# Layer-0 output projection and gate transposes moved to the two transpose banks, probabilities in two buffers, orders laid anew

## The chip, the cores and the metric

One core of one Trainium2 chip runs the whole program. The time is device microseconds of one execution, lower is better. The engines are TensorE (PE), VectorE (DVE), ScalarE (ACT), GpSimd (POOL) and the queue engine SyncE (SP). They run side by side, each takes its instructions strictly in the order in which they were written, and they wait for one another on semaphores. TensorE writes its results to PSUM, of which this kernel uses eight banks of 512 float32 columns.

## The reference

Four sequences of 512 tokens, 128 channels, and a context of 77 tokens for each. Two layers, all in float32, here with the names of the steps in the kernel:

```python
# layer 0, attention over the context: 16 heads of 8
q = LN(x) @ Wq.T + bq;  k, v = ctx @ Wk.T + bk, ctx @ Wv.T + bv        # hstats hnorm hturn hq
p = softmax(q k^T / sqrt(8))                                            # s mx sub exp
x = x + (p v) @ Wo.T + bo                                               # ta tb tc, v nm, ot op x
# layer 0, second half: attention among the 4 sequences, 4 heads of 32, then a mixture of 8 experts
z = LN(x);  z = z + MHA_over_the_batch(z);  y = LN(z) * g1 + b1         # zturn q qk dot soft wv tot mturn proj res ynorm
gates = softmax(y @ wg);  e = argmax;  place in e's queue, cap 256      # yturn lg gdiff gate places cap
x = x + LN(y + gate * (y @ w1[e] + b1[e]) @ w2[e] + ...) * g2 + b2      # load turn moe total norm2
# layer 1, attention over the context with the 32 largest scores of each head
s = LN(x) Wq1 ctx Wk1                                                   # lturn ask scores keep
p = softmax(s where s >= 32nd largest);  x = x + p ctx                  # max mark dif cut exp sign product, turn copy value norm add3
# layer 1, token-shifted channel mixing
z = LN(x);  out = x + sigmoid(mix_r(z) W_r) * (relu(mix_k(z) W_k)^2 W_v)   # fturn shift up acts down half end
```

## The kernel before

The 2048 tokens are 16 tiles of 128. Layer 0's attention and the part among the sequences go by `j` (0 to 3), the quarter of the sequence, with the four sequences together, since a token attends to the same position of the other three. Inside `attend(j)` a tile has the number `u = 4 j + b`. Everything later goes by tile `t` (0 to 15). `ORDER` is one list of some 2200 words such as `v1@2` (step `v1` at index 2), written out by hand or by a tool. Each engine's block goes through that list (`run`) and issues those steps that belong to it. So the list fixes the order on every engine. What may not run yet waits on a semaphore (`hold`).

The names that matter here:

- `psS` is four PSUM banks with the scores. `psT[:, 0]` and `psT[:, 1]` are the two transpose banks. `psM0` and `psM1` are the last two.
- In `attend`, `s{b}` makes the scores, `mx{b}` and `sub{b}` (DVE) take the maximum and subtract it, `exp{b}` (ACT) makes `e0`. `ta`, `tb`, `tc` transpose `e0` in ten pieces into the banks of `psT`, `ca`, `cb`, `cc` (ACT) copy them to `pT`, and `v{b}` multiplies them with the values into `psM0`. `nm{b}` (DVE) divides, `ot{b}` transposes the result, `oT{b}` copies it, `op{b}` is the output projection and `x{b}` (DVE) adds it to `x1`. Before the change `ot` and `op` write to `psM0` too, so `m0_free` lets the next `v`, `hturn` or `hq` into `psM0` only when `x{b}` is done (`x1_made`).
- `among(j)` works in `psM1`: `zturn`, `q0` to `q3`, `mturn`, `proj`, then `yturn`, `lg` and `places` for the gates. `zturn` of the next `j` waits for `gates_set`, the last of them.
- `topk(t)` on DVE is 16 steps `max..` and 12 steps `mark..` of four heads each. It finds the 32 largest of 77 scores per head. `keep@t` (ACT) brings the scores of tile `t` to it, from a ring of four buffers. `cut`, `dif` and `product` (POOL) and `exp`, `sign` (ACT) make the probabilities, `turn0` to `turn2` and `value` multiply them, `norm@t` (DVE) inverts the denominators.
- `mix(t)` is `fturn`, `shift`, `up`, `acts`, `down`, `fvalue`, `half`, `end`. Its work lies in `psT[:, 1]`.
- `fill@k` is two matmuls of ones on a mask row, into `psT[:, 1]`, whose result nobody reads. There are 420 of them, spread over the list.

Statistics of the layer norms on DVE use the tiles `stats`, `mv`, `veps`, `rstd` under a key `x` or `m`. The two norms of `among` share the key `m`.

## Time and profile before

| | us |
|---|---|
| median of 3 runs | 541.65 |
| fastest, slowest of them | 537.23, 545.12 |
| span of the profiled execution | 543.1 |
| DVE busy in it | 477.4 (88%) |
| PE busy in it | 471.0 (87%) |
| ACT, POOL busy | 294.5, 263.8 |

The profiled execution is one of its own. Its span is counted from its first to its last instruction; its time on the device's counter isn't listed. The span lies inside the range of the three times and 1.45 us above their median. Busy times are those in which at least one instruction of the engine was under way. On PE they hold the fills too.

### The profile page before, as it was taken

To read this page: it belongs to the slowest core of one execution; us is meant where nothing else is said; L and a number is where in the kernel's file an instruction comes from. 1 tells how busy PE (TensorE), PEld (TensorE's weight loads), DVE (VectorE), ACT (ScalarE), POOL (GpSimd) and SP (SyncE) were. 2 spreads that over 40 slices of the span, in tenths; PEclk is the share of its full clock that TensorE was granted. 3 is DMA by queue.
4 is the path that set the end of the run, shared out by engine and by line. 5 is a ranking of instruction groups with operands and counts; after the bars stand their busy time and mean duration, and the time that the engine had idled before them with its cause. 6 is when DMAs were issued, how large, how long until landed. Compare 5 with 4: busy or idle time off the path is not lost. (4 is left out here: it accounts for less than half of the span.)

```text
span 543.1 us, 12113 instructions
## 1 busy us (share of the span) xinstructions
PE 471.0 (87%) x3161; PEld 347.3 (64%) x3161; DVE 477.4 (88%) x3011; ACT 294.5 (54%) x812; POOL 263.8 (49%) x403
## 2 busy tenths in 40 slices
PE   4999999898986999799889898999889989689485
PEld 3578877566755765467657666667657757566374
DVE  5784679959879899899989999999999999999972
ACT  1143551433444335424777788787786887635343
POOL 4320120500323435634685687777668667736622
PEclk9999999979998999899999999999999998989957
DMA  8700000000000000000000000000000000000000
GB/s 278 301 2 1 2 1 2 0 1 0 2 2 0 2 2 1 1 1 2 7 1 8 7 2 2 10 2 2 11 1 2 7 7 7 2 5 8 6 5 11
DMA packets 5938, 9.68 MB, mean 18 GB/s; under 512 B 744, under 2 KB 4976, under 8 KB 5616
## 3 DMA queue, kind: packets, MB, share of 16 engines
q1 hardware_dynamic: 5584, 8.35, 4.3%
q8 instruction: 28, 0.46, 0.4%
q10 hardware_dynamic: 288, 0.56, 0.3%
q14 instruction: 38, 0.31, 0.2%
HBM read 7.86 MB, written 1.05 MB: 16 GB/s over the span
## 5 line engine op out<-in xcount | busy, mean ns | idle before, releaser
L1318 PE MATMUL psT<-mrow,mones 128*128 128x308 bf16 x840 | 131.3, 303 | 5.0 <-ACT vv L672 4.3
L939 DVE MAX8 top<-area_b 128x8 f32<-128x77 f32 x768 | 116.0, 290 | 0.0
L1318 PEld LDWEIGHTS psT<-mrow,mones 128*128 128x128 bf16 x840 | 83.6, 101 | 41.2 <-issue 14.7
L947 DVE MATCH_REPLACE8 area_b<-top,area_b 128x77 f32<-128x77 f32 x512 | 109.1, 293 | 0.0
L947 DVE MATCH_VALUE_LOAD area_b<-top,area_b 128x8 f32 x512 | 74.2, 150 | 0.0
L947 DVE MATCH_REPLACE8 area_b<-top,area_a 128x77 f32<-128x77 f32 x256 | 54.7, 286 | 0.0
L1088 PE MATMUL psM<-vblk,pT 128*128 128x135 f32 (+3 forms) x320 | 42.4, 288 | 5.2 <-ACT early L562 3.0
L1088 PEld LDWEIGHTS psM<-vblk,pT 128*128 128x128 f32 (+1 forms) x320 | 39.7, 197 | 8.9 <-issue 7.2
L420 POOL TENSOR_TENSOR p<-area_b 128x1232 f32<-128x1232 f32 x15 | 41.9, 2792 | 6.9 <-issue 3.3
L1286 PE MATMUL psM<-vblk,pT 128*128 128x135 f32 (+3 forms) x320 | 43.5, 292 | 1.5 <-ACT pT L631 0.8
L1286 PEld LDWEIGHTS psM<-vblk,pT 128*128 128x128 f32 (+1 forms) x320 | 41.2, 203 | 5.1 <-issue 4.3
L319 POOL TENSOR_TENSOR rstd_m<-veps_m,expo 128x4 f32<-128x4 f32 x8 | 8.1, 1018 | 74.7 <-DVE veps_m L689 74.4
L581 ACT ACTIVATE mparts<-psM,cur 128x128 f32<-128x128 f32 x128 | 38.1, 369 | 9.8 <-PE psM L1225 9.6
L939 DVE MAX8 top<-area_a 128x8 f32<-128x77 f32 x256 | 38.3, 285 | 5.0 <-ACT area_a L609 5.0
L1269 PE MATMUL psT<-consts,p 128*128 128x128 f32 (+1 forms) x160 | 29.0, 299 | 14.6 <-POOL p L420 8.9
L413 POOL TENSOR_TENSOR area_b<-area_a,top 128x1232 f32<-128x1232 f32 x15 | 34.0, 2266 | 12.0 <-DVE top L939 9.9
L406 POOL TENSOR_TENSOR dif<-area_a,top 128x1232 f32<-128x1232 f32 x16 | 36.3, 2268 | 4.6 <-DVE top L939 4.6
L947 DVE MATCH_VALUE_LOAD area_b<-top,area_a 128x8 f32 x256 | 35.5, 143 | 0.0
L716 DVE TENSOR_REDUCE mx<-psS 128x16 f32<-128x1232 f32 x16 | 23.0, 1438 | 13.5 <-PE psS L1059 13.4
L1233 PE MATMUL psM<-mparts,consts 128*128 128x128 f32 x288 | 34.8, 275 | 0.0
L1269 PEld LDWEIGHTS psT<-consts,p 128*128 128x128 f32 (+1 forms) x160 | 18.3, 146 | 25.2 <-POOL p L420 11.3
L1233 PEld LDWEIGHTS psM<-mparts,consts 128*128 128x128 f32 x288 | 33.4, 192 | 0.0
(223 smaller groups left out, 1015.0 us busy)
## 6 DMA issues: line engine op xcount, KB each, us to landing
area_a<-in_w1T SPq DMA_DIRECT2D x1, 2064.0 KB, 11.0
area_b<-in_w SPq DMA_DIRECT2D x1, 2048.0 KB, 15.4
x<-in_x SPq DMA_DIRECT2D x4, 256.0 KB, 6.9
out<-fin SPq DMA_DIRECT2D x16, 64.0 KB, 1.5
rows<-in_rows SPq DMA_DIRECT2D x1, 576.0 KB, 6.7
vblk<-in_vblk SPq DMA_DIRECT2D x1, 540.0 KB, 15.6
weights<-in_weights SPq DMA_DIRECT2D x1, 516.0 KB, 6.5
consts<-in_consts ACTq DMA_DIRECT2D x1, 392.5 KB, 3.9
```

The lines of the kernel that those rows point to most:

```text
L406: e.tensor_tensor(dif[:], scores_sb[t % RING][:], top[:, t % 2, 0, :, 0, None].broadcast_to([P, H, KEYS]), ALU.subtract)\
L413: e.tensor_tensor(cut, scores_sb[t % RING][:], top[:, t % 2, TOPK // 8 - 1, :, 7, None].broadcast_to([P, H, KEYS]), ALU.subtract)\
L420: e.tensor_tensor(p1.rearrange("p (h k) -> p h k", k=KEYS), ex1, cut, ALU.mult).then_inc(s["p_set"], 1)
L581: ins = e.activation(mparts[:, x_], psM0[:, at + (x_ - lo) * D:at + (x_ - lo + 1) * D], ACT.Copy, scale=cur[:, D + x_:D + x_ + 1])
L716: e.tensor_reduce(mx0.rearrange("p (g i) -> p g i", g=G), scores_ps, AX, ALU.max).then_inc(s["s_max"], 1)
L939: ins = e.max(tops[:, r, h], (left if r else scores_sb[t % RING])[:, h])
L947: ins = e.match_replace(left[:, h], tops[:, r, h], (left if r else scores_sb[t % RING])[:, h], GONE)
L1088: ins = mm(streams(psM0, c), pT[0:w, c], vblk0[0:w, b, c, None, :].broadcast_to([w, copies(c)[0], VB]), start=(c == 0), stop=(c == NCH - 1 ...
L1233: ins = mm(psM0[:, 0:D], ident, mparts[:, x_], start=False, stop=(x_ == E))
L1269: ins = tr(psT[0:w, 0, (c % 4) * P:(c % 4 + 1) * P], p1[:, c * P:c * P + w], ident)
L1286: ins = mm(streams(psM1, c), pT1[0:w, c], vblk1[0:w, t // NJ, c, None, :].broadcast_to([w, copies(c)[0], VB]), start=(c == 0), stop=(c == ...
L1318: mm(bank[:, 0:B * KEYS], mones[:], mrow.rearrange("p b k -> p (b k)"), start=True, stop=True)
```

## The change

1. `ot{b}` and `op{b}` write to `psT[:, 1]` (columns 256 and 384) and no longer to `psM0`, and `x{b}` reads there. `psM0` is free for the next user when `nm{b}` has read the product (`pv_norm`).
2. `yturn`, `lg` and `places` write to `psT[:, 0]` and no longer to `psM1`. The copy of the transposes goes to a tile of its own, `yT`. `zturn` of the next `j` waits for `m_res`, the residual, and no longer for the gates.
3. `pT` has two buffers, so `ca` and `cb` wait for the product of the tile before the last and no longer for the last.
4. The waits for the transpose banks stand in two functions, `t0_free` and `t1_free`. All users of such a bank wait for all earlier ones: `tb`, `ot`, `op`, `fturn` and `fill` for the adds `x{b}`, `ta` and `turn0` for the gates.
5. The norm of `ynorm` has tiles of its own (key `y`), and one semaphore counts the three steps of the statistics. In `gdiff` two instructions change places.
6. `FILLS` is 355 and no longer 420, and `ORDER` is another list. In front of `max00@0`, the first top-k step, it has 8 fills, where the old one had 55. The numbers of all other instructions stay the same.

```diff
-FILLS = 420
+FILLS = 355
...
+STATS = 2 * B + 1
...
-        for n in ("x", "m"):
+        for n in ("x", "m", "y"):
...
-        pT = sb("pT", [P, NCH, P])
+        pT = sb("pT", [P, 2, NCH, P])
...
+        yT = sb("yT", [P, B, P])
...
         def m0_free(e, step):
             hold(e, s["h_xnT"], begun(step, "hturn"))
             hold(e, s["h_qT"], begun(step, "hq"))
-            hold(e, s["x1_made"], begun(step, "v0", "v1", "v2", "v3"))
+            hold(e, s["pv_norm"], begun(step, "v0", "v1", "v2", "v3"))
             hold(e, s["n2_out"], begun(step, "turn"))
+
+        def t0_free(e, step):
+            hold(e, s["t_copiedA"], 3 * begun(step, "ta0", "ta1", "ta2", "ta3"))
+            hold(e, s["p_copied"], 3 * begun(step, "turn0"))
+            hold(e, s["y_T"], begun(step, "yturn"))
+            hold(e, s["g_d"], begun(step, "lg"))
+            hold(e, s["gates_set"], begun(step, "places"))
+
+        def t1_free(e, step):
+            projected = begun(step, "op0", "op1", "op2", "op3")
+            hold(e, s["x1_made"], projected)
+            if projected < NT:
+                hold(e, s["t_copiedB"], begun(step, "tb0", "tb1", "tb2", "tb3"))
+                hold(e, s["o_T"], begun(step, "ot0", "ot1", "ot2", "ot3"))
+            hold(e, s["f_vv"], begun(step, "fturn"))
...
                     def first():
-                        hold(e, s["pv_made"], u)
+                        hold(e, s["pv_made"], u - 1)
                         hold(e, s["t_turned"], 3 * u + 1)
-                        e.activation(pT[:, 0:4].rearrange("p c n -> p (c n)"), psT[:, 0], ACT.Copy).then_inc(s["t_copiedA"], 1)
+                        e.activation(pT[:, u % 2, 0:4].rearrange("p c n -> p (c n)"), psT[:, 0], ACT.Copy).then_inc(s["t_copiedA"], 1)
...
+                def upright():
+                    hold(e, s["y_turned"], j + 1)
+                    hold(e, s["lg_made"], j)
+                    e.activation(yT[:], psU, ACT.Copy).then_inc(s["y_T"], 1)
...
-                        e.tensor_tensor(x1[:, t], psM0[:, 384:512], x1[:, t], ALU.add).then_inc(s["x1_made"], 1)
+                        e.tensor_tensor(x1[:, t], psT[:, 1, 384:512], x1[:, t], ALU.add).then_inc(s["x1_made"], 1)
...
                     def oturn():
                         hold(e, s["pv_norm"], u + 1)
-                        tr(psM0[:, 256:384], at0[:], ident).then_inc(s["o_turned"], 1)
+                        t1_free(e, f"ot{b}@{j}")
+                        tr(psT[:, 1, 256:384], at0[:], ident).then_inc(s["o_turned"], 1)
 
                     def project():
                         hold(e, s["o_T"], u + 1)
-                        mm(psM0[:, 384:512], at0T[:], Wt["wo0"], start=True, stop=True).then_inc(s["o_proj"], 1)
+                        t1_free(e, f"op{b}@{j}")
+                        mm(psT[:, 1, 384:512], at0T[:], Wt["wo0"], start=True, stop=True).then_inc(s["o_proj"], 1)
...
                 def zturn():
                     if j == 0:
                         e.wait_ge(s["b12_stored"], 1)
-                    hold(e, s["gates_set"], j)
+                    hold(e, s["m_res"], j)
                     hold(e, s["q_z"], B * j + B)
                     turn4(psM1, zt, s["q_turned"])
...
-ORDER = """hstats@0 masks@0 hrstd@0 kblk1@0 hnorm@0 vb0@0 kblk@0 hturn@0 vb1@0 keys@0 hT@0 bias@0 vm0@0 hq@0 hstats@1 hqT@0 s0@0 vm1@0 hrstd@1
+ORDER = """hstats@0 hrstd@0 hnorm@0 masks@0 bias@0 hturn@0 kblk@0 hT@0 vb0@0 kblk1@0 hq@0 hstats@1 vb1@0 keys@0 hqT@0 vm0@0 hrstd@1 wmix@0
```

Three places of the order. The first is PE at its start. L1112 (after: L1136) spreads the values of layer 0, L1031 (L1055) transposes the normalised tokens, L1043 (L1067) makes the queries, L1056 and L1059 (L1080, L1083) the scores, L1318 is a fill. Before:

```order
L1112 MATMUL psM<-vsrc,consts 128x4x24 x5
L1031 MATMUL psM<-consts,xn 128x128 x4
L1112 MATMUL psT<-vsrc,consts 128x4x24 x5
L1043 MATMUL psM<-hT,early 128x512
L1056 MATMUL psS<-kblk,hT 128x308 x4
L1059 MATMUL psS<-mrow,mones 128x308 x4
L1318 MATMUL psT<-mrow,mones 128x308 x18
L1056 MATMUL psS<-kblk,hT 128x308 x4
L1059 MATMUL psS<-mrow,mones 128x308 x4
```

After:

```order
L1055 MATMUL psM<-consts,xn 128x128 x4
L1136 MATMUL psM<-vsrc,consts 128x4x24 x5
L1067 MATMUL psM<-hT,early 128x512
L1136 MATMUL psT<-vsrc,consts 128x4x24 x5
L1080 MATMUL psS<-kblk,hT 128x308 x4
L1083 MATMUL psS<-mrow,mones 128x308 x4
L1055 MATMUL psM<-consts,xn 128x128 x4
L1067 MATMUL psM<-hT,early 128x512
L1080 MATMUL psS<-kblk,hT 128x308 x4
L1083 MATMUL psS<-mrow,mones 128x308 x4
```

The transposes and the queries moved ahead of the spreading, those of the second quarter stand where the 18 fill matmuls stood. The second place is PE at the end of quarter 1 of the attention. L1088 (L1110) is the product `v`, L1095 (L1118) is `ot`, L1099 (L1123) is `op`, L1077 (L1099) the transposes of `e0`. Before:

```order
L1088 MATMUL psM<-vblk,pT 128x5x27 x6
L1056 MATMUL psS<-kblk,hT 128x308 x4
L1059 MATMUL psS<-mrow,mones 128x308 x4
L1077 MATMUL psT<-consts,e 128x128
L1077 MATMUL psT<-consts,e 80x128
L1095 MATMUL psM<-consts,at 128x128
L1318 MATMUL psT<-mrow,mones 128x308 x4
L1099 MATMUL psM<-early,at0T 128x128
L1318 MATMUL psT<-mrow,mones 128x308 x6
L1088 MATMUL psM<-vblk,pT 128x3x27 x2
```

After:

```order
L1110 MATMUL psM<-vblk,pT 128x5x27 x6
L1099 MATMUL psT<-consts,e 128x128
L1099 MATMUL psT<-consts,e 80x128
L1123 MATMUL psT<-early,at0T 128x128
L1110 MATMUL psM<-vblk,pT 128x3x27 x2
L1110 MATMUL psM<-vblk,pT 128x4x27 x2
L1110 MATMUL psM<-vblk,pT 128x5x27 x6
L1080 MATMUL psS<-kblk,hT 128x308 x4
L1083 MATMUL psS<-mrow,mones 128x308 x4
L1099 MATMUL psT<-consts,e 128x128 x4
L1118 MATMUL psT<-consts,at 128x128
L1123 MATMUL psT<-early,at0T 128x128
```

A product now follows the one before it without the transpose and the projection of that tile between them, and the fills there are gone. The third place is POOL after the top-k of tile 14. L413 (L433) is `cut@14`, L406 (L426) `dif@15`, L420 (L440) `product@14`, L429 and L437 (L449, L457) are `aproduct@13` and `add3@13`, L447 (L467) is `half`, L452 and L455 (L472, L475) are `end`. Before:

```order
L447 TENSOR_SCALAR er<-er 128x128
L452 TENSOR_TENSOR vv<-vv,er 128x128
L455 TENSOR_TENSOR fin<-x3,vv 128x128
L413 TENSOR_TENSOR area_b<-area_a,top 128x1232
L406 TENSOR_TENSOR dif<-area_a,top 128x1232
L429 TENSOR_TENSOR att1<-avs,rden1 128x128
L437 TENSOR_TENSOR x3<-x2,att1 128x128
L420 TENSOR_TENSOR p1<-area_b 128x1232
```

After:

```order
L433 TENSOR_TENSOR area_b<-area_a,top 128x1232
L426 TENSOR_TENSOR dif<-area_a,top 128x1232
L472 TENSOR_TENSOR vv<-vv,er 128x128
L475 TENSOR_TENSOR fin<-x3,vv 128x128
L440 TENSOR_TENSOR p1<-area_b 128x1232
L449 TENSOR_TENSOR att1<-avs,rden1 128x128
L467 TENSOR_SCALAR er<-er 128x128
L457 TENSOR_TENSOR x3<-x2,att1 128x128
```

`end@12` stood ahead of `cut@14` and now stands behind `product@14`, and `product@14` no longer stands behind `aproduct@13` and `add3@13`. On DVE, `norm@14` stood ahead of the last step `max33@15`; now two steps `mark`, four steps `max` and a part of the last product stand between them. Four fill matmuls stand ahead of the last product of tile 15 and 18 ahead of its `fturn`, where there were none.

## Rows read from the trace of the kernel before

**Rows 1.** All engines in five stretches (stretch, its length, busy us of each engine, granted clock)

```profile
...
core 0: us, PE busy (x) PEld busy (x) DVE busy (x) ACT busy (x) POOL busy (x), PEclk, DMA share, GB/s
0.00:30.00 30.00, 21.62 (x98) 14.55 (x98) 19.22 (x56) 7.23 (x12) 12.06 (x27) 1.00 0.71 262
30.00:178.25 148.25, 133.17 (x941) 100.48 (x942) 115.20 (x256) 60.52 (x131) 29.95 (x46) 0.96 0.01 1
178.25:330.00 151.75, 138.28 (x944) 100.29 (x944) 143.60 (x1049) 86.68 (x255) 86.88 (x125) 0.99 0.01 3
330.00:503.30 173.30, 154.39 (x1057) 112.97 (x1057) 173.30 (x1465) 125.46 (x371) 119.67 (x182) 0.97 0.02 5
503.30:543.10 39.80, 23.52 (x128) 19.00 (x126) 26.08 (x189) 14.59 (x44) 15.26 (x24) 0.76 0.03 7
```

**Rows 2.** Waits of DVE: line, what it waited for, us in total, times, longest

```profile
...
DVE mx L716 <- PE psS L1059: 13.4, 9, 3.8
DVE rden L728 <- PE psM L1088: 7.7, 4, 4.9
...
DVE top L939 <- ACT area_a L609: 5.0, 4, 2.8
```

**Rows 3.** PE busy with the fills (L1318) alone, in three of these stretches

```profile
...
0.00:30.00 30.00, 5.12 (x22) 1.00 0.71 262
30.00:178.25 148.25, 14.38 (x88) 0.96 0.01 1
...
330.00:503.30 173.30, 54.22 (x354) 0.97 0.02 5
```

**Rows 4.** Timeline of PE, start (start us, us, line, what, idle before)

```profile
...
14.66 1.91 PE L1112 MATMUL psT<-vsrc,consts 77*128 77x96 f32 x8
16.36 1.97 PE L1043 MATMUL psM<-hT,early 128*128 128x512 f32 x2
19.20 1.41 PE L1056 MATMUL psS<-kblk,hT 32*128 32x308 f32 x8 [0.87 <-ACT hT L481]
...
21.55 4.42 PE L1318 MATMUL psT<-mrow,mones 128*128 128x308 bf16 x18
```

**Rows 5.** Timeline of PE, one handing over of psM0

```profile
...
128.33 0.49 PE L1099 MATMUL psM<-early,at0T 128*128 128x128 f32 x2
129.74 2.55 PE L1088 MATMUL psM<-vblk,pT 128*128 128x81 f32 x20 [0.92 <-DVE x L737]
```

**Rows 6.** Timeline of DVE, the steps between them

```profile
...
127.20 0.29 DVE L731 TENSOR_TENSOR at<-psM,rden 128x128 f32<-128x128 f32 x1
...
129.21 0.28 DVE L737 TENSOR_TENSOR x<-psM,x 128x128 f32<-128x128 f32 x1
```

**Rows 7.** Stretches around two falls of the granted clock

```profile
...
104.50:109.30 4.80, 1.87 (x15) 1.63 (x13) 4.57 (x16) 0.39 (x2) 3.38 (x6) 0.79 0.00 0
109.30:114.00 4.70, 4.70 (x18) 2.25 (x18) 1.07 (x1) 1.28 (x2) 0.30 (x1) 0.50 0.00 0
506.40:516.20 9.80, 2.75 (x20) 1.82 (x20) 9.80 (x88) 3.61 (x7) 8.91 (x7) 0.86 0.03 8
516.20:527.20 11.00, 10.04 (x41) 8.60 (x41) 7.96 (x59) 4.39 (x12) 2.21 (x7) 0.50 0.02 6
...
536.20:543.10 6.90, 2.93 (x11) 2.18 (x11) 0.69 (x3) 0.98 (x5) 1.20 (x3) 0.59 0.08 21
```

**Rows 8.** Timeline of POOL, tail

```profile
...
507.31 2.27 POOL L413 TENSOR_TENSOR area_b<-area_a,top 128x1232 f32<-128x1232 f32 x1
...
513.43 2.78 POOL L420 TENSOR_TENSOR p<-area_b 128x1232 f32<-128x1232 f32 x1
```

**Rows 9.** Timeline of PE, tail

```profile
...
522.59 4.61 PE L1286 MATMUL psM<-vblk,pT 128*128 128x81 f32 x20
```

**Rows 10.** Timeline of DVE, tail

```profile
...
503.33 2.48 DVE L939 MAX8 top<-area_a 128x8 f32<-128x77 f32 x16
...
527.24 0.26 DVE L973 RECIPROCAL rden<-psM 128x16 f32<-128x16 f32 x1 [2.78 <-PE psM L1286]
```

362 lines of the change are left out of this document (182 added, 180 removed).

## The prediction

> **What bounds the kernel now.** I read the table of stretches first, then the waits of DVE, then timelines where those waits are long. The table [rows 1] cuts the span where the first top-k step begins (178.25 us), where DVE stops having gaps (330) and where the top-k of the last tile begins (503.3). In each stretch, length less DVE's busy time is DVE's idle time: 10.8, 33.1, 8.2, 0.0 and 13.7 us, 65.7 in all. From 330 to 503.3 the reader is to see that DVE has no gap. So DVE bounds that stretch, and nothing that PE gains or loses there counts unless DVE starves. The change leaves DVE's work as it is, one instruction for one. The time after is therefore DVE's 477.4 us busy plus the idle time that is left, and the sum is one over the four stretches with idle time.
>
> PE is a second bound ahead of 178.25. From 30 to 178.25 it is busy 133.2 of 148.3 us, of which the fills are only 14.4 [rows 1, 3]. What DVE waits for is PE's results [rows 2]: the scores (13.4 us, nine times), the product of a tile (7.7 us), and, later, ACT's copy of the scores to the top-k (5.0 us). Those waits follow from how banks are handed over. At one place, the operation `nm` starts its second half at 127.20 [rows 6], the projection `op` starts at 128.33 [rows 5], `x` on DVE starts at 129.21 [rows 6], and only then the next product begins, at 129.74 [rows 5], after PE stood idle for 0.92 us. Bank `psM0` was tied up for 2.5 us though its product had been read by 127.49.
>
> **The sum, part by part**, against the span of 543.1 us.
>
> *The start (0 to 30 us).* Before, the second half of the spread begins at 14.66, the queries at 16.36 and the first scores at 19.20 [rows 4]. Afterwards the normalised tokens are turned ahead of both halves of the spread, and the queries ahead of the second. The second half took 16.36 - 14.66 = 1.7 us, and the first half is as large, so up to 3.4 us leave the path to the first scores, less what else those wait for (the key blocks on DVE, not in my rows). DVE now has the small mixing products ahead of its first maximum, where it was idle anyway. I take -3, bounds -3.4 and 0. The 18 fills that began at 21.55 and ran 4.4 us lay in PE's wait for the first exponentials; I cost their loss at nothing.
>
> *The attention and the middle part (30 to 178.25).* Three edits work on the same gaps: `psM0` is freed after `nm`, `psM1` after the residual, and the second `pT` lets ACT copy while the last product runs. No row gives their price alone. One bound is the idle time of DVE there, 33 us; a tied-up bank of some 2.5 us once per tile of 16 would give 40, so it is no tighter. The other bound is 0, if DVE's and PE's chains through the scores bank `psS` (maximum, subtract, next scores) set the pace, which the change doesn't touch. Between them stands the order itself: PE's real work ahead of `max00@0` is the same in both lists, but 44 fills of this stretch (88 matmuls, 14.4 us, 0.163 us each [rows 3]) and 11 earlier ones have become 8, or 16 x 0.163 = 2.6 us. A fill only stands where PE would have had to wait. If PE's other waits stay as they are, this stretch shortens by 14.4 - 2.6 = 11.8 us. I take -11: it is nearest to a count of instructions, and it leaves DVE 22 of its 33 us idle.
>
> *What that costs.* First, new waits. `tb`, `ot` and the fills now wait for the add `x` of every earlier tile, and PE issues in order, so scores and products queue behind. The add takes 0.28 us [rows 6], but DVE may be in a maximum. A wait of the length of the one that goes (0.92 us) at each of 16 tiles would be 15 us; where DVE is early it is nothing. I take +1. Second, the clock. Between 104.5 and 109.3 PE was busy 1.87 of 4.8 us, and in the 4.7 us after that the granted clock was 0.50, that is 1.2 instead of 2.4 GHz; DVE got only 1.07 us of work done in them [rows 7], so such a fall costs about 3.6 us. With 47 fills fewer ahead of the top-k there can be more of them, but there are also fewer gaps. I take +2, bounds 0 and +11 (three more).
>
> The Trainium skill ("TensorE: Matmul & The Clock Gate", Part 1, "What's actually happening") says that the throttled state is the default and activity releases it. That speaks against a list with 65 fills fewer, and by it the head could keep the half clock for long; rival B says what that would cost here. The trace agrees so far as a fall follows a stretch of little work [rows 7].
>
> *The first top-k tiles (178.25 to 330).* DVE is idle 8.2 us [rows 1], of which 5.0 are four waits for the copy `keep`, the longest 2.8 [rows 2]. In the new list `keep@4` and `keep@5` stand some ten top-k steps ahead of their use, before they stood one or two ahead; `keep@0` and `keep@3` stay close. I take -2, bounds -5 and +3 (one more wait like the longest).
>
> *The tail (503.3 to the end).* `cut@14` can start when tile 14's top-k is over, at 503.33 [rows 10], but started at 507.31 [rows 8], since POOL had `end@12` ahead of it, which waits for PE. Afterwards nothing of that kind is ahead of it: up to 4.0 us earlier, and `product@14` no longer stands behind `add3@13`. But DVE only waits 2.78 us for that chain, at `norm@14` [rows 10], and this step now stands six top-k steps and one part earlier. A top-k tile has 160 instructions on DVE, so 1465 of them in 173.3 us make 19.0 us a tile [rows 1] and 0.68 for each of its 28 steps: six are 4.1 us. So the 4 us are needed for staying even, and at full clock one more: the value product took 4.61 us at clock 0.50 [rows 7, 9], where the same kind of 20 matmuls takes 2.55 at full clock [rows 5]. Behind the last product, the mixing of tile 14 is now out of the way, and 18 fills stand ahead of the last transpose. PE ran at 0.59 there [rows 7], 2.9 us busy; at full clock that is some 1.2 us less. If the clock is low the fills themselves take 18 x 0.245 = 4.4 us (as at 21.55 [rows 4]) and push the end back by 1 to 2 us. I take -3, bounds -6 and +2.
>
> Sum: -3 - 11 + 1 + 2 - 2 - 3 = -16, or 527.1 us against the span. The span lies 1.45 us above the median of the runs, so I expect **526 us**, 2.9% less than 541.65. The three runs spread over 7.9 us; about 2% is what a measurement of this kernel can tell from no change. That band is 530.8 to 552.5.
>
> **Rivals.**
>
> A. *The gain is given back in the head.* PE's order stalls on `x1_made` and clock falls take the fills' place: three more falls (11 us) or 0.7 us a tile on the adds. That leaves -16 + 9 to 11, or 534 to 538 us. For it: a granted clock of 0.50 over whole stretches with DVE idle [rows 7], and eight fills where 55 were. Against it: over the whole stretch from 30 to 178.25 the granted clock was still 0.96 with fills for 14.4 us of 148 [rows 1, 3].
>
> B. *Slower, by the clock.* PE stays at half clock in much of the head because nothing fills its gaps. Its real work from 30 to 178.25 is 133.2 - 14.4 = 118.8 us [rows 1, 3], and a value product grows from 2.55 to 4.61 us, a factor of 1.8. Each us of PE's work at half clock adds 0.8 us while PE sets the pace. So the gain of 16 us is gone when 20 us of that work run at half clock, and 40 us (a third) give 526 + 32 = 558 us. In the top-k stretch the same gives little: real PE work is (154.4 - 54.2) / 9.1 tiles = 11.0 us a tile [rows 1, 3], 19.8 at half clock, against DVE's 19.0. Against it: once PE is slow it is busy all the time, as at 109.3 to 114.0 [rows 7], and the clock came back after each such fall.
>
> C. *The handing over was most of it.* DVE's idle time from 30 to 178.25 falls to 8 instead of 22 us, since three banks are freed early and DVE's work can be pulled forward: 512 us. For it: PE's and DVE's real work there are 118.8 and 115.2 us, both well under 148. Against it: the scores chain through the one set of `psS` banks.
>
> D. *The change doesn't do what it says*: in this stretch `psS` sets the pace and the old list had fills simply in its gaps. The head stays, and only start, top-k and tail give -8 + 3: 537 us, a part of the same range as A.
>
> **How the numbers follow.** My forecast's own range is 518 to 531, chance 0.60. A and D together 0.23 (532 to 540). B 0.08 (above 552). C 0.09 (below 518). The range 513 to 539 takes in most of A, D and C and leaves out B and the ends. Faster by over 2%: 0.60 + 0.09, less a little of the forecast's upper end, 0.68. Within 2%: 0.24. Slower by over 2%: 0.08.
>
> **What would show it.** The first `max00` starts at about 163 to 166 us. DVE's first maximum starts at 18 to 19 us and no longer 21.79. In the waits of DVE, those for the product and the scores fall by half. From some 300 us on DVE has no gap until the last tile. DVE's busy time stays at 477 us, the fills' falls from 131 to about 110. If waits for `x` on PE, or a granted clock under 0.9 in the head, show more than 5 us, rival A was right. If DVE has gaps after 330 us, my belief that the top-k stretch is safe was wrong.

## The result and the profile after

The changed kernel takes 538.72 us (median of 20 runs, 533.06 to 545.56); the kernel before took 541.90 us beside it (20 runs, 536.93 to 545.12). The ratio is 0.992, 95% interval [0.989, 0.995]: faster by 0.8%, inside the band of 2% that counts as the same, where I had forecast 2.9%. Here and below the ratios leave out runs that count as slow (4 of these 20), which the medians take in, so a ratio is not the quotient of the two medians (0.994 here). The profiled execution has a span of 534.5 us and took 536.31. It is a good one of its kind (granted clock 0.952, where the 20 runs average 0.945), so its span is 8.6 us under that of [rows 1] while the medians are 3.2 us apart.

The table of stretches, cut as [rows 1] at the first top-k step (now 160.6 us) and at the first maximum of the last tile (now 497.4); the cut at 330 is the same time, not the same event. Its columns are those of [rows 1].

```profile
core 0: us, PE busy (x) PEld busy (x) DVE busy (x) ACT busy (x) POOL busy (x), PEclk, DMA share, GB/s
0.00:30.00 30.00, 19.95 (x110) 14.23 (x110) 21.69 (x74) 9.01 (x14) 14.26 (x32) 0.89 0.73 263
30.00:160.60 130.60, 114.21 (x847) 88.85 (x843) 108.69 (x228) 59.06 (x131) 27.68 (x41) 0.99 0.01 1
160.60:330.00 169.40, 143.11 (x898) 104.51 (x899) 158.30 (x1155) 97.29 (x289) 95.67 (x139) 0.92 0.01 3
330.00:497.40 167.40, 148.53 (x1017) 109.32 (x1018) 162.11 (x1370) 113.61 (x332) 108.77 (x166) 0.97 0.02 5
497.40:534.50 37.10, 25.04 (x166) 18.71 (x164) 25.16 (x187) 15.40 (x48) 16.93 (x28) 0.95 0.03 10
```

The head is 178.25 - 160.6 = 17.6 us shorter and the tail 39.8 - 37.1 = 2.7 us. But the two stretches of the top-k together are 169.4 + 167.4 = 336.8 us, where they were 325.05: 11.8 us longer. From 330 on DVE stands idle for 5.3 us, where it had no gap at all. The granted clock from the first top-k step to 330 us is 0.92, where it was 0.99: by the mean, some 27 of the 169.4 us were at the lower of the two levels, before some 3 of 151.75.

The waits of DVE over the whole span, to be read against [rows 2] (line 997 was 973, line 741 was 716, line 753 was 728):

```profile
DVE rden L997 <- PE psM L1314: 12.5, 3, 6.0
DVE mx L741 <- PE psS L1083: 10.3, 9, 2.2
DVE rden L753 <- PE psM L1110: 6.9, 7, 2.4
...
DVE rden L1002 <- PE psM L1314: 4.6, 1, 4.6
```

The first row is the one that grew (3.3 us before). It is the step `norm` of the top-k tiles, which waits for `value`, the product with the turned probabilities. The timeline of PE (line 1314) has the products of tiles 4 and 8:

```profile
317.38 2.48 PE L1314 MATMUL psM<-vblk,pT 128*128 128x81 f32 x20
...
410.65 2.48 PE L1314 MATMUL psM<-vblk,pT 128*128 128x81 f32 x20
```

and that of DVE (line 997) the two norms behind them, with the idle time in brackets:

```profile
319.90 0.26 DVE L997 RECIPROCAL rden<-psM 128x16 f32<-128x16 f32 x1 [5.98 <-PE psM L1314]
...
413.16 0.26 DVE L997 RECIPROCAL rden<-psM 128x16 f32<-128x16 f32 x1 [5.29 <-PE psM L1314]
```

The two stalls are 11.3 us. They can be followed in VectorE's first maximum of each tile: tile 5 begins at 295.32 us (before at 313.05, so 17.7 us sooner), tile 6 at 320.59 (11.5 sooner), tile 11 at 421.10 (6.1 sooner), and the last at 497.26 (6.1 sooner). The same product of tile 8 in the timeline of PE of the kernel before:

```profile
410.43 2.48 PE L1286 MATMUL psM<-vblk,pT 128*128 128x81 f32 x20
```

VectorE reaches tile 8 some 12 us sooner than before, and TensorE delivers that tile's values at the same microsecond. That row is the riddle: who holds the values back?

### The profile page after: what moved, and what is told of

It is laid out like the page before. It is cut to its first block, busy times and chain, and to the rows that moved or that the text cites. A ratio compares the mean times of both kernels' runs of the same rounds, so it can differ in the third digit from the quotient of the medians.

```text
span 534.5 us, 11794 instructions
## 1 busy us (share of the span) xinstructions
PE 450.8 (84%) x3031; PEld 335.6 (63%) x3031; DVE 475.9 (89%) x3011; ACT 294.4 (55%) x812; POOL 263.3 (49%) x403
## 4 chain that ended last, share of the span: by engine, by line
PE 35%; DVE 34%; ACT 11%; POOL 10%; issue 9%; DMA 1%; ACTq 0%; POOLq 0%; DVEq 0%
DVE area_b L971 9%; DVE top L963 9%; PE psM L1314 4%; PE psM L1110 4%; PE psM L1261 3%; PE psT L1345 3%; ACT mparts L606 3%; PE psM L1253 3%; POOL p L440 2%; PE psM L1248 2%; POOL area_b L433 2%; DVE mx L741 2%; ACT area_b L646 2%; DVE d L746 2%; PE psT L1099 2%
## 5 line engine op out<-in xcount | busy, mean ns | idle before, releaser
L1345 PE MATMUL psT<-mrow,mones 128*128 128x308 bf16 x710 | 113.7, 308 | 3.6 <-ACT vv L697 2.4
L963 DVE MAX8 top<-area_b 128x8 f32<-128x77 f32 x768 | 113.5, 239 | 0.0
L971 DVE MATCH_REPLACE8 area_b<-top,area_b 128x77 f32<-128x77 f32 x512 | 107.6, 240 | 0.0
L1345 PEld LDWEIGHTS psT<-mrow,mones 128*128 128x128 bf16 x710 | 71.9, 103 | 36.9 <-issue 12.4
L971 DVE MATCH_VALUE_LOAD area_b<-top,area_b 128x8 f32 x512 | 49.6, 97 | 0.0
L1314 PE MATMUL psM<-vblk,pT 128*128 128x135 f32 (+3 forms) x320 | 43.0, 290 | 4.1 <-ACT avs L671 1.6
L606 ACT ACTIVATE mparts<-psM,cur 128x128 f32<-128x128 f32 x128 | 38.2, 369 | 13.7 <-PE psM L1253 13.5
L1314 PEld LDWEIGHTS psM<-vblk,pT 128*128 128x128 f32 (+1 forms) x320 | 40.3, 199 | 7.8 <-issue 7.2
L440 POOL TENSOR_TENSOR p<-area_b 128x1232 f32<-128x1232 f32 x15 | 41.9, 2794 | 3.5 <-issue 3.3
L1110 PE MATMUL psM<-vblk,pT 128*128 128x135 f32 (+3 forms) x320 | 40.6, 281 | 1.3 <-DVE at L756 0.6
L1110 PEld LDWEIGHTS psM<-vblk,pT 128*128 128x128 f32 (+1 forms) x320 | 38.6, 192 | 3.5 <-issue 1.5
L433 POOL TENSOR_TENSOR area_b<-area_a,top 128x1232 f32<-128x1232 f32 x15 | 34.0, 2267 | 13.6 <-DVE top L963 13.6
L426 POOL TENSOR_TENSOR dif<-area_a,top 128x1232 f32<-128x1232 f32 x16 | 36.3, 2268 | 4.7 <-DVE top L963 4.7
L741 DVE TENSOR_REDUCE mx<-psS 128x16 f32<-128x1232 f32 x16 | 23.0, 1438 | 10.4 <-PE psS L1083 10.3
L1253 PE MATMUL psM<-w,y1T 128*128 128x512 f32 (+1 forms) x64 | 25.8, 485 | 5.8 <-ACT mparts L606 5.6
L393 POOL TENSOR_TENSOR lrs<-lvar,expo 128x1 f32<-128x1 f32 x47 | 26.1, 556 | 3.9
## 6 DMA issues: line engine op xcount, KB each, us to landing
area_a<-in_w1T SPq DMA_DIRECT2D x1, 2064.0 KB, 11.3
```

The lines of the kernel that those rows point to most:

```text
L426: e.tensor_tensor(dif[:], scores_sb[t % RING][:], top[:, t % 2, 0, :, 0, None].broadcast_to([P, H, KEYS]), ALU.subtract)\
L433: e.tensor_tensor(cut, scores_sb[t % RING][:], top[:, t % 2, TOPK // 8 - 1, :, 7, None].broadcast_to([P, H, KEYS]), ALU.subtract)\
L440: e.tensor_tensor(p1.rearrange("p (h k) -> p h k", k=KEYS), ex1, cut, ALU.mult).then_inc(s["p_set"], 1)
L606: ins = e.activation(mparts[:, x_], psM0[:, at + (x_ - lo) * D:at + (x_ - lo + 1) * D], ACT.Copy, scale=cur[:, D + x_:D + x_ + 1])
L963: ins = e.max(tops[:, r, h], (left if r else scores_sb[t % RING])[:, h])
L971: ins = e.match_replace(left[:, h], tops[:, r, h], (left if r else scores_sb[t % RING])[:, h], GONE)
```

## The experiments

Eighteen kernels ran on the chip, in five rounds on four chips. Each round had the kernel before beside it (medians 541.55, 541.16, 541.67, 543.30 and 541.15 us), and ratios are to it, so kernels of different rounds are best compared by their ratios. All spans and waits are of one profiled execution.

One warning for reading them: the 14 kernels with the new order have the same list up to the first top-k step, yet it starts anywhere from 160.6 to 165.8 us in their profiles. In the first 160.6 us the granted clock was 0.97 in the changed kernel and 0.91 in e3_fills. So the 17.6 us by which the head is shorter is the best of 14 profiles. The middle one has 16.4, the last 12.5, and a time later in a profile carries that shift with it.

**1. Is it VectorE's order, a queue, or the clock?** Three easings of the changed kernel at the two stalls. In the lists (steps between those shown are left out):

```diff
 # e1_late: further back
-... value@4 ... norm@4 max33@5 acopy@4 aproduct@4 ...
+... value@4 ... norm@4 mark13@6 acopy@4 aproduct@4 ...
-... norm@8 square4@7 turn@14 max20@10 ...
+... max20@10 ... mark22@10 norm@8 mark23@10 acopy@8 ...
 # e2_source: further ahead
-... scale4@2 half@1 keys@7 cut@4 ...
+... cut@4 scale4@2 half@1 keys@7 ...
-... moe2@13 ... total@13 ... value@8 ...
+... value@8 moe2@13 ... total@13 ...
 # e3_fills: 13 fills, 355 to 368
+turn0@3 fill fill fill fill fill fill fill ... turn1@3
+total@12 fill fill fill fill fill fill ... fturn@6
```

> The changed kernel with the norm of tile 4 and the norm of tile 8 (and the two small steps that follow each) further back in the lists, behind some 10 us and 4.8 us of the next tile's top-k work on VectorE; nothing else moves. Theory 1 (the norms stand too early on VectorE, which alone sets the pace): the stalls of 5.98 us at 319.90 and 5.29 us at 413.16 go, apart from about 0.5 us of the second, and nothing takes their place; tiles 5 and 10 of the top-k take 19.1 us instead of 25; the span falls from 534.5 by 10 to 11 us, to about 524. Rival (TensorE and GpSimd are themselves late there, and VectorE meets the lateness at the next step that it waits for, the scores or the next norm): at most half comes back, the span is 529 or more, and other waits of VectorE grow by the rest.

Measured: 535.56 us (10 runs), ratio 0.990 [0.986, 0.993]. The stall at tile 4 is gone, the one at tile 8 is not, though its norm stands 4.8 us of work further back. Timeline of DVE, line 997:

```profile
417.86 0.26 DVE L997 RECIPROCAL rden<-psM 128x16 f32<-128x16 f32 x1 [6.66 <-PE psM L1314]
```

and of POOL, the cuts of tiles 7 and 9 (whose top-k had ended at 357.3 and 395.2):

```profile
367.44 2.26 POOL L433 TENSOR_TENSOR area_b<-area_a,top 128x1232 f32<-128x1232 f32 x1
...
404.86 2.27 POOL L433 TENSOR_TENSOR area_b<-area_a,top 128x1232 f32<-128x1232 f32 x1
```

The rival's mechanism held, and more than half did not come back. VectorE ran tiles 5 to 9 at 19.05 us each; the cuts, which had been up to 6.0 us late in the changed kernel, were now up to 10.2 us late, and the values of tiles 4 to 8 came every 23.3 us, as they had in the changed kernel. The values of tile 8 end 252.8 us after the first top-k step, in the changed kernel 252.5. VectorE had only run further ahead of the others. (This profile is of the longest of the ten runs, 540.32 us, and its first top-k step is at 165.0.)

> The norms stay where they are; what they wait for comes sooner. On GpSimd the cut of tile 4 goes ahead of the four small steps that held it (it started at 301.43, its input was ready at 295.43); on TensorE the values of tile 8 go ahead of the expert work of tile 13, with the copy that frees their buffer moved up on ScalarE. If the lateness is that of in-order queues, the cut of tile 4 starts at about 296, its values end by 315 instead of 319.86, and those of tile 8 end by 404 instead of 413.12: VectorE's wait for values falls from 12.5 us to under 3, the span to 525 to 528. If the lateness came from the half-rate clock alone, with no queue at fault, the values move by under 2 us and the span by under 2.

Measured: 539.72 us (10 runs), ratio 0.999 [0.995, 1.002]. The cut did start early (297.63 us instead of 301.43, in a profile whose first top-k step came 2.4 us later), and the gain was lost one step on. Timeline of POOL, cut and product of tile 4:

```profile
297.63 2.27 POOL L433 TENSOR_TENSOR area_b<-area_a,top 128x1232 f32<-128x1232 f32 x1 [2.35 <-DVE top L963]
...
308.27 2.79 POOL L440 TENSOR_TENSOR p<-area_b 128x1232 f32<-128x1232 f32 x1
```

The product came 10.6 us behind its cut instead of 5.6, since the steps that had been passed now stood between them: POOL waited 0.94 us for the input of one of them, and later 2.26 us for `load`. The values of tile 8 ended at 408.7, 4.4 us sooner, and the norm then waited for a GpSimd step instead (3.59 us). VectorE's waits for values fell from 12.5 to 9.3 us, not under 3 as expected. Moving one step ahead had moved another back.

> 13 more fillers, 7 behind the first turn of tile 3 (where TensorE idled from 285.2 to 287.25) and 6 ahead of the fturn of tile 6 (idle 394.8 to 396.0 behind it); one small ScalarE step moved so that the first 7 may run. Clock theory: the granted clock stays at 1.00 from 288.8 to 299.0 and from 398.0 to 404.9, where it was 0.50; the cut of tile 4 starts by 298, VectorE's wait for values falls from 12.5 us to 3 to 6, the span to 526 to 530. Rival (the clock falls anyway, or the fillers delay the turns by as much, 1.8 and 1.6 us at full rate): the wait stays at 10 us or more and the span within 2 us of 534.5.

Measured: 535.60 us (9 runs), ratio 0.987 [0.983, 0.991]. Stretches of this kernel at the places where the clock had fallen (0.50 and 0.51 in the changed kernel), and where it fell instead (the clock is 1.00 also in these two stretches moved by the 5.1 us that this profile's first top-k step is later):

```profile
288.80:299.00 10.20, 8.37 (x62) 6.66 (x61) 10.20 (x89) 8.45 (x29) 6.84 (x20) 1.00 0.03 9
398.00:404.90 6.90, 4.89 (x26) 3.00 (x26) 6.90 (x61) 4.56 (x20) 4.12 (x9) 1.00 0.01 2
328.00:334.90 6.90, 5.83 (x23) 4.02 (x24) 6.90 (x63) 3.72 (x11) 5.97 (x10) 0.51 0.00 0
```

The first stall shrank from 5.98 to 1.58 us, as the clock theory says; the second grew from 5.29 to 6.34, behind a fall at 328 us that lasts 6.9 us. VectorE waited 9.8 us for values in all, between the two cases. The medians of this kernel and of e1_late (535.56) lie some 3 us under that of the changed kernel, and the intervals of all three overlap: neither gain is clear of noise.

> The changed kernel without the 13 fillers that stand in TensorE's list between the norm of tile 12's expert output and the values of tile 8 (342 of 355 stay). The run with the norms set back showed that, with the stall at tile 4 gone, VectorE runs tiles 5 to 9 at 19.05 us each while the values of tiles 4 to 8 follow at 23.3 us each: the others are late, and VectorE meets it at tile 8. If TensorE's queue is what is late there, 13 fillers of 0.26 us at full rate and 0.5 us at half rate are 3.4 to 6.8 us of it: the values of tile 8 end at 407 to 409 instead of 413.12 and the stall of 5.29 us falls to under 2; the span falls by 3 to 5 us. Rival (clock): without them the clock stays at half rate longer than the 6.8 us at 398, the expert work takes back what the fillers gave, and the stall stays within 1 us of 5.29.

Measured: 540.38 us (10 runs), ratio 1.000 [0.996, 1.003]. The stall at tile 8 became 5.98 us, and the half-rate stretch there 10.2 us instead of 6.8. That is the rival's outcome: the clock took back what leaving out the fills gave.

> All of it together: the norms of tiles 4 and 8 set back, the cut of tile 4 and the values of tile 8 brought forward, 7 fillers behind the first turn of tile 3, the 13 fillers ahead of the values of tile 8 left out. If the stalls are lateness that accumulates in the queues of TensorE and GpSimd between tiles 4 and 8, both stalls go (VectorE's wait for values under 2 us beside the last tiles), tiles 1 to 14 of the top-k take 19.1 us each once the head's work is done, and the median is 528 to 532, that is 0.975 to 0.982 of before. If every easing only lets VectorE run into the same lateness later (at tiles 11 to 14), the median stays at 534 or more.

Measured: 541.21 us (10 runs), ratio 0.999 [0.995, 1.003]. This is the second case: the stall at tile 4 is gone, that at tile 8 is 5.09 us, and a new one of 6.27 us stands at tile 11. Its last tiles' values came when they came in e1_late (the values of tile 14 ended at 517.8 and 517.7 us), though VectorE had reached tile 10 some 3.4 us sooner.

> The two easings that each gave about 3 us, together: the norms of tiles 4 and 8 set back and the 13 fillers more. If their gains add, the median ratio to before is 0.983 to 0.985 (532 to 534 us). If both only move the point at which VectorE meets the other engines, it is 0.987 to 0.990, as each alone.

Measured: 538.55 us (10 runs), ratio 0.993 [0.989, 0.996]. The gains of the norms and of the fills do not add, and by the ratio not even one of them is left, which is beyond both cases. No version that computes the whole result beats the changed kernel by more than the intervals leave open.

**2. What did the banks do by themselves?** The kernel before in its old order, with parts of the change:

```diff
 # e7_pt: two buffers of turned probabilities, nothing else
-pT = sb("pT", [P, NCH, P])
+pT = sb("pT", [P, 2, NCH, P])
-hold(e, s["pv_made"], u)
+hold(e, s["pv_made"], u - 1)
 # e4_banks: that, and the projection in psT[:, 1], with its waits
-mm(psM0[:, 384:512], at0T[:], Wt["wo0"], start=True, stop=True)
+t1_free(e, f"op{b}@{j}")
+mm(psT[:, 1, 384:512], at0T[:], Wt["wo0"], start=True, stop=True)
-hold(e, s["x1_made"], begun(step, "v0", "v1", "v2", "v3"))
+hold(e, s["pv_norm"], begun(step, "v0", "v1", "v2", "v3"))
 # e8_headfill: e4_banks without 45 fills between tb0@0 and turn@0
```

> The kernel before, in its old order, with one part of the change alone: the turned probabilities in two buffers, so that the copies of a head group need not wait for the product before. Nothing else moves. The part alone removes waits of ScalarE only; TensorE waited 0.8 us in all for these copies' buffers, and VectorE's 7.7 us for the products came from the handover of the bank. Expected: first top-k step at 176 to 178.3, the time within 2 us of before. If this wait was the one that held the head, the first top-k step comes at 172 or sooner and the time falls by 4 us or more.

> The kernel before, in its old order (one ScalarE step, the copy of a turned head, moved behind one copy of turned probabilities), with three parts of the change: the layer-0 projection and its turn in the second transpose bank, the turned probabilities in two buffers, and the handover of the first product bank at the norm instead of at the residual sum. The gates stay in their old bank, and all 420 fillers stay. If the banks make the gain of the head by themselves, the first top-k step comes at 166 or sooner (178.25 before, 160.64 after) and the span is 532 or less. If the order makes it, it comes at 174 or later and the span is 539 to 545. My own sum had 11 us for these waits and none for the order: by it 167. I now expect 173, since in the changed kernel much stands earlier in the lists.

> The banks in the old order again (555 us, first top-k step at 190.9), now without the 45 fillers of the head that stand between the first turn into the second transpose bank and the first turn of the experts. In that run fillers waited 2.5 us for the copy of the turned head and 1.5 us for the residual sum, and VectorE 7.3 us for the projection. If the fillers' new waits on the shared bank made the loss, the first top-k step comes back to 180 or sooner and the median to 545 or less. If it is the projection and the turns that wait for one another in one bank, the first top-k step stays at 186 or later. A third case: the clock falls for want of fillers (more than 20 us of half rate in the head, where 17 us stood), and the step comes no sooner either, with the granted clock of 30 to 180 under 0.9.

Measured: e7_pt 541.55 us, ratio 1.000 [0.997, 1.004], first top-k step at 178.8: nothing, as expected. e4_banks 554.97 us (4 runs), ratio 1.028 [1.022, 1.034], first top-k step at 191.0: these banks in the old order make the kernel 13 us slower, and the step comes far behind the 173 us that I expected. "174 or later" held, the span (556.6 us) is beyond the 539 to 545 that went with it. What DVE waits for in its head, from 26 to 178 us, where before it waited 1.2 us for the projection:

```profile
DVE mx L724 <- PE psS L1067: 11.4, 10, 3.2
DVE qkv L811 <- PE psM L1170: 8.5, 8, 2.3
DVE rden L736 <- PE psM L1095: 7.4, 3, 5.2
DVE x L745 <- PE psT L1108: 7.3, 7, 1.7
```

In a bank that the turns, the projection and the fills share, each waits for the other's reader. On PE the turn `ot` and the projection wait 3.0 and 2.7 us for the copy of the turned probabilities, the turns `tb` and the fills 1.6 and 2.5 us for the copy of the turned head, and the fills 1.5 us for `x`. It is the kind of loss that my rival A named, though only the last is its wait for `x`. Without the head's fills (e8_headfill) the median is 558.37 us, ratio 1.032 [1.026, 1.038], and the first top-k step is at 189.5: the fills' waits were not the loss. The granted clock from 30 to 189 us was 0.90, so the third case cannot be parted from the second. What can be said is that none of these parts shortens the head in the old order. The new order needs the new banks: of the 15 tiles after the first, the copies `ca` of 11 and `cb` of 8 stand ahead of the product `v` of the tile before, and that product mostly (11 of 14) ahead of the `x` of the tile before it, which one buffer and the old bank forbid. That the head's gain comes from this pairing is the reading that is left; no run has the new order without a bank, and the gates' move to the other bank was in none of the three runs.

**3. Does VectorE set the pace at all?** The easing, in both kernels; the other heads take their maxima from the whole scores:

```diff
+def marked(h):
+    return t in (0, 1, LASTT) or h % HG == 0
-for h in range(g * HG, g * HG + HG):
+for h in filter(marked, range(g * HG, g * HG + HG)):
     ins = e.match_replace(left[:, h], tops[:, r, h], ...)
```

> The changed kernel with less work on VectorE and nothing else altered: in tiles 2 to 14 of the top-k only one head in four has its eight largest struck out between rounds (12 strikings a tile instead of 48), and the other heads take their maxima from the whole scores each round, so that the result is another one. A tile then costs VectorE about 64 x 0.141 + 12 x 0.209 = 11.5 us instead of 19.05, 98 us less in all. If VectorE is what the top-k stretch goes by (my prediction's premise), the span falls from 534.5 to 440 to 460. If the other engines, following their lists, have a pace of their own of 21 to 23 us a tile there, as the values of tiles 4 to 8 did with the norms set back, the span stays above 505 and VectorE stands idle for most of what was taken away.

> The kernel before with the same easing of VectorE (result altered in the same way). It gives the pace of the other engines in the old order. If the gain of the head was given back because the other engines need as long from the start to the end in the new order as in the old, this span and that of the eased changed kernel are within 5 us of one another. If the new order gave the other engines no pace of its own to fall back on (the old order could go as slowly), this one is longer than the other by 10 us or more, about what the head gained.

Measured: e9_lite 540.34 us (10 runs), ratio 0.996 [0.992, 1.001]; e10_litebefore 540.04 us (10 runs), ratio 0.995 [0.992, 0.999]. VectorE was busy 381.0 us instead of 475.9 in the one and 381.2 instead of 477.4 in the other, and neither kernel became faster by more than 2 us. Its waits in e9_lite from 160 us on:

```profile
DVE rden L1000 <- PE psM L1317: 83.5, 9, 24.2
DVE top L966 <- POOL area_b L433: 13.2, 4, 6.1
DVE top L966 <- ACT area_a L634: 10.3, 2, 8.3
```

and in e10_litebefore from 178 us on:

```profile
DVE rden L976 <- PE psM L1289: 82.3, 12, 9.1
DVE top L942 <- ACT area_a L609: 15.5, 5, 7.9
```

The spans are 537.7 and 539.6 us: in e9_lite the second case (above 505), far from the 440 to 460 us of my premise, and in e10_litebefore the first (within 5 us of the other). All of the work taken away came back as waiting. The values of tile 8 in e10_litebefore, in the timeline of PE:

```profile
408.23 2.48 PE L1289 MATMUL psM<-vblk,pT 128*128 128x81 f32 x20
```

They ended at 410.7 against 412.9 in the kernel before. So also before the change, in the stretch where DVE had no gap [rows 1], the other engines ran at almost exactly the same pace by themselves, and both orders let them finish at the same time.

**4. Which of the others?** On top of e9_lite, one engine eased at a time from tile 4 on:

```diff
 # e13_pool: dif, cut and product
+n = H if t < 4 else H // 2
-e.tensor_tensor(dif[:], scores_sb[t % RING][:], ...
+e.tensor_tensor(dif[:, 0:n], scores_sb[t % RING][:, 0:n], ...
 # e14_act: exp, Relu and the kept scores by halves, and
-for x_ in range(lo, hi):
+for x_ in range(lo, hi if t < 4 else (lo + hi + 1) // 2):
 # e15_pe: turn0 and turn1 by halves, and
-lo, hi = ((3, 7), (7, 8))[n - 1]
+lo, hi = ((3, 7 if t < 4 else 5), (7, 8))[n - 1]
-for x_ in range(E + 1):
+for x_ in range(E + 1 if t < 4 else 3):
```

> The eased changed kernel (e9_lite, median 540.3) with GpSimd's three large steps of a tile (the two differences and the product) done for half of the heads from tile 4 on: (2.27 + 2.27 + 2.79) / 2 = 3.67 us a tile, 40 us in 11 tiles (the result is altered again). If GpSimd is a link of the chain that sets the pace, as its 12% of the chain of the eased kernel says, the median falls by 12 us or more. If the chain is held by TensorE's list and GpSimd's work lies beside it, by under 4 us.

> The eased changed kernel with ScalarE's work cut from tile 4 on: the copy of the scores, the exponential and the last step of the sign for half of the heads, and 5 of 8 expert copies: 0.6 + 0.6 + 0.6 + 3 x 0.3 = 2.7 us a tile, 32 us in 12 tiles (the result is altered). ScalarE has 15% of the chain: if it is a link, the median falls by 8 us or more; if not, by under 3 us.

> The eased changed kernel with TensorE's work cut from tile 4 on: 3 of 9 terms of the experts' sum, 2 of 4 experts in the middle product, 4 of 10 turns of the probabilities left out: 0.73 + 0.42 + 0.44 = 1.6 us a tile at full rate, 19 us in 12 tiles (the result is altered). TensorE has 45% of the chain: if its list is what holds the others, nearly all of it comes back, 12 us or more, as long as the granted clock stays near 0.937; if the clock falls with the work, part of it is lost again, about 2.7 us for each hundredth of the clock, as the 20 runs of the changed kernel give it. If TensorE is no more of a limit than the others, under 5 us.

Measured, 4 runs each: 534.51 us, ratio 0.989 [0.981, 0.997]; 534.20, 0.988 [0.980, 0.995]; 534.33, 0.988 [0.980, 0.996]. By the medians each gives about 6 us over e9_lite, for 40, 32 and 19 us of work taken away; but e9_lite ran in another round, and by the ratios (0.996 [0.992, 1.001] for it) it is 4 to 5 us each, with intervals that overlap. None reached the mark that I had set for a link of the chain; whether they stayed under the other mark the noise leaves open. The mean clock of the runs of e15_pe was 0.914, against 0.937 in e9_lite; at 2.66 us a hundredth (the slope of the time over the clock in the 20 runs of the changed kernel, where 0.919 gave 544.7 us and 0.962 gave 534.1) that is another 6 us, so TensorE may have the largest share; that is an estimate, no run keeps the clock up. These runs single out no engine. That the limit is the path of a tile's steps through three in-order lists fits them and is not shown by them.

> The eased changed kernel without the 72 fillers between the values of tile 4 and those of tile 10. At full rate they are 18.7 us of TensorE. If they stand in the way of the others' chain, the span is shorter than that of the eased kernel by 8 to 18 us; if they run while TensorE waits anyway, or if the clock then falls and takes it back, the two are within 3 us.

> The changed kernel, its whole result, with 44 fillers more (399; 420 stood before), two ahead of each of the second and third turns and of the values of tiles 3 to 13, where these wait. Clock theory: over its 20 runs the changed kernel lost 2.66 us for each hundredth of the granted clock, its mean clock is 0.945 against 0.961 before; with the fillers the mean clock is 0.955 or more and the median 534 to 536. If TensorE's own queue is the limit, 44 fillers of 0.26 us cost it 11 us of which over half shows, and the median is 543 or more in spite of the clock.

Measured: without 72 fills 546.68 us (10 runs), 6.3 us slower than e9_lite, the mean clock of its runs 0.913 against 0.937. That is outside both of my cases: at 2.66 us a hundredth the lower clock alone is worth an estimated 6.4 us, the whole loss, so that leaving out the fills gave nothing beside it. With 44 fills more on the real kernel 540.26 us (10 runs), mean clock 0.953, ratio 1.003 [0.998, 1.009]. Half of the clock came back and the time did not: by the ratios it is 1.1% slower than the changed kernel (0.992 [0.989, 0.995]), and the intervals do not touch. So 44 fills cost TensorE's list more than the clock returned.

**5. Is the head's gain still there?** All three others eased as above, but for the kept scores, with VectorE's work whole, in both kernels.

> The changed kernel with VectorE's work whole and the three others eased together from tile 4 on: the halved differences and product on GpSimd (3.7 us a tile), the halved exponential and sign step and 5 of 8 expert copies on ScalarE (2.1 us), fewer expert products, sum terms and turns on TensorE (1.6 us); the result is altered. If the others' shared chain is what took back the gain of the head, VectorE now runs nearly without a gap from 160.6 us on: its waits for values fall from 12.5 us to under 4 and the median is 524 to 530, the time that I had forecast for the real kernel. If VectorE's own order is at fault, it stays at 535 or more.

> The kernel before with the same three easings. Before, VectorE had next to no gap from 313 to 503 us, so that easing the others gives it little there: 534 to 540. If so, this one minus the eased changed kernel is 9 to 15 us, the head's gain come through. If the difference stays at 3 to 5 us, as between the real kernels, the gain of the head is lost for another reason than the others' pace.

Measured: e17_others 528.86 us (4 runs, 528.26 to 529.43), ratio 0.976 [0.970, 0.982]; e18_othersbefore 542.59 us (10 runs), ratio 1.005 [1.001, 1.009]. They are 13.7 us apart where the real kernels are 3.2 us apart. Waits of DVE in e17_others from 160 us on:

```profile
DVE rden L1002 <- PE psM L1319: 6.0, 3, 3.8
DVE rden L1007 <- PE psM L1319: 4.6, 1, 4.6
```

The stall at tile 8 is 0.5 us there, and that at tile 4, where the easing only begins, 3.84. The first expectation held for the time; the waits for values fell to 6.0 us, not under 4. The second held for the difference and not for the time, which is above 540. With the others out of the way the change is worth 2.5%, near the size that I had forecast. Easing them in the kernel before gives nothing: its VectorE is busy 175.2 of the 175.2 us from 330 us to its last tile (505.2 us) in e18_othersbefore too. The mean clocks of the two kernels, 0.918 and 0.925, are alike, so the 13.7 us are not the clock's.

## Why the prediction was wrong

The step that failed is the first conclusion of its first part: "So DVE bounds that stretch, and nothing that PE gains or loses there counts unless DVE starves." From DVE without a gap between 330 and 503.3 us [rows 1] I concluded that the others had room. A full row of one engine tells that it is not waiting; it does not tell by how much the others are ahead. e10_litebefore shows that they had about 2 us of room (540.04 against 541.67 us): VectorE and the chain through the other three engines were both limits of some 540 us. The change shortened the one by some 14 us (e18_othersbefore less e17_others) and left the other where it was (540.34 us in e9_lite).

Its sum, term by term. The prediction added up idle time of DVE on the premise that DVE's work stays where it is, so each term has two measures, the stretch and DVE's idle time in it:

- *The start*, -3: DVE's first maximum is at 18.48 us instead of 21.79, 3.3 us sooner. DVE's idle time up to 30 us went from 10.8 to 8.3. Right.
- *Attention and middle*, -11, with +1 and +2 for new waits and the clock, -11 with the start in all: the first top-k step came 17.6 us sooner, but DVE's idle time ahead of it fell by 13.6 us (43.8 to 30.2). The other 4.0 us are work put behind that step: DVE is busy 130.4 us ahead of it instead of 134.4. "PE's real work ahead of `max00@0` is the same in both lists" was misread: `mturn@2`, `tot3@2`, `tb3@3` and the gates of quarter 1 (`lg@1` to `places@1`) stood ahead of it and now stand behind, while `v2@3`, `nm2@3` and `ot2@3` came ahead. From 30 us on the idle time went from 33.1 to 21.9, as the -11 says; what I had set aside for waits and clock did not come in this profile. The granted clock was 0.99 there; PE waited 1.8 us in all for the copy of the turned head and for `x` too little to be listed. The count of fills held (19.5 us ahead of the first top-k step before, 3.2 after), but that their going makes the gain is not shown: e8_headfill left out 45 of them, with the banks in the old order, and its first top-k step came only 1.5 us sooner than in e4_banks. I had credited the banks' waits, too; those for scores and product fell only from 13.4 to 10.3 and from 7.7 to 6.9 us, not by half, and e7_pt and e4_banks show that these parts give nothing or a loss without the order.
- *The top-k tiles*, -2, bounds -5 and +3 for the first ones and nothing for the rest: measured +11.8 up to the last tile, of which 8.2 us are idle time (8.2 before, 16.4 after, the two stalls 11.3 of them) and 3.5 us the work put behind the first top-k step. This is the term that was wrong, by the premise above. The wait for `keep` did go, as I had said (5.0 to 0.4 us). The clock term stood in the wrong stretch: it was for the head, and the clock fell behind it, in the first top-k tiles (0.92 instead of 0.99), where I had priced it at nothing. e3_fills, with the clock kept up in two places, has the first stall at 1.58 instead of 5.98 us.
- *The tail*, -3: measured -2.7 (DVE's idle time 13.7 to 11.9), right in size. The norm of tile 14 waits 1.23 us instead of 2.78.
- The fills' busy time is 113.7 us (forecast about 110), DVE's 475.9 (forecast 477).

These sum to -17.6 + 11.8 - 2.7 = -8.5 us for the profiled pair (8.6 before rounding). The medians differ by 3.2 only, as the pair flatters the change from both ends: its profiled run of after lies 2.4 us under the median (536.31 against 538.72), and the span of before, 543.1, with the 1.8 us that lie around a span in after (536.31 less 534.5) lies some 3 us above 541.90.

Of the rivals, A and D together named the right size (532 to 540) for the wrong places: A's stalls in the head did not come, and D had the head stay where it was. B had worked out that half clock in the top-k stretch "gives little", from 11.0 us of real work a tile against 19.0. That was the same error in other clothes: work per engine was compared with VectorE's pace, and by that measure the others have room, while e9_lite and e10_litebefore show that together they take as long as VectorE. The path of a tile through the in-order lists is how I explain it; no run shows that path by itself. I had also written "If DVE has gaps after 330 us, my belief that the top-k stretch is safe was wrong"; it has 5.3 us of them.

What stays open: why the two orders give the other engines' chain the same end within 1 us. TensorE's work without fills is 337.1 us after and 339.7 before, but that is not a sum that explains 540. That the lists were laid to keep the others just ahead of VectorE would fit; no run tests it. A part may be the clock: e9_lite ran at a mean of 0.937 and e10_litebefore at 0.962, which at 2.66 us a hundredth is an estimated 6.6 us, so at one clock the new order's chain could be the shorter one. No run has both at the same clock; e16_more, which raised it by fills in the changed kernel, gained nothing.

## What to carry to other kernels

When one engine has no gap, ask how much later its suppliers would be if it were faster: take work away from it in one run, even if the result is then another one, and see whether the time moves. If it does not, there is a second limit of the same size, and a gain on the first is worth only the difference. Where engines follow fixed lists, the second limit may be the path through several of them, each only half to five sixths busy; then, as in the seven easings here that kept the whole result, moving a single step or a filler can shift the stall rather than remove it. And look at the granted clock of every profile before comparing times in two of them: the same list took 160.6 to 165.8 us to its first top-k step.

## What was not expected of the hardware

More fillers were not better, nor were fewer. In the changed kernel the clock fell to half after a stretch in which TensorE was busy 1.27 of 3.8 us:

```profile
285.00:288.80 3.80, 1.27 (x10) 0.77 (x8) 3.80 (x35) 3.69 (x9) 2.80 (x9) 1.00 0.00 0
288.80:299.00 10.20, 9.58 (x38) 8.12 (x37) 10.20 (x86) 5.64 (x26) 4.32 (x13) 0.50 0.02 7
```

With thirteen more fillers at two places it stayed at 1.00 there, and fell at 328 us instead; 13 fewer, 44 more and (in the eased kernel) 72 fewer each gave nothing or cost time. And a lower clock reached the end only in part: a hundredth less of the mean over 535 us is 5.3 us of TensorE's work at full rate, and over the 20 runs of the changed kernel the time grew by 2.66 us, about half.
